# Cross network on one core: VectorE's products spread over the tile, rows and fetches begun earlier, one fp32 chunk where three stood

## The chip, the core and the metric

The kernel runs on one core of a Trainium2 chip. The metric is the device time of one execution in microseconds (us), the median of several runs. Five engines work side by side, each through its own list of instructions in order, and wait for one another on semaphores: TensorE (PE; its weight loads are shown apart as PEld), VectorE (DVE), ScalarE (ACT), GpSimd (POOL) and SyncE (SP), which here only issues DMAs. "SPq" in a row is SP's queue of DMA issues.

## What is computed

512 samples, 39 features each, every feature a row of 16 numbers fetched from its own table. Three layers follow, of 128 maps each, and then a small dense network:

```python
e = stack([tbl_f[ids[:, f]] for f in range(39)])        # (512, 39, 16)
x0 = xk = e
for W in (f0, f1, f2):                                  # (39*39,128), (128*39,128), (128*39,128)
    z = einsum('bfd,bgd->bfgd', x0, xk).reshape(b, f*g, d)
    xk = einsum('bpd,pm->bmd', z, W); outs.append(xk)
h = concatenate([sum(concatenate(outs), -1), dense_ctx], 1)
y = relu(relu(h @ W_top1 + b1) @ W_top2 + b2) @ W_top3  # (512, 1)
```

## The kernel before, in words

**Tiles and slots.** The samples are cut into 16 tiles of 32 samples, which are 512 columns (sample times 16). A tile's second layer is 40 "banks" (`SLOTS`), one for four features of one block of 128 columns; the bank is also the clock of the whole schedule. "Slot s of tile t" (written t:s) is the place of bank 40t+s in each engine's list. What stands at slot s on an engine comes after the engine's work for bank s, in program order; no engine waits for a slot as such, only for its data. `layer2` on TensorE multiplies x1 (split into a high and a low part) with the filter (split as well) in three matmuls, lines 900 to 902, into one of four PSUM buffers (`RING`). Bank n may start when bank n-4 has been read. ScalarE reads banks 0, 3 and 6 of every ten (`scale_bank`, line 594), VectorE the other seven (`add_bank`, line 802: four `scalar_tensor_tensor` per bank, each scaling by a value of x0 and adding to what ScalarE or the bank before left). GpSimd folds a block's sums at slots 8 and 12 of each ten (`fold_two` line 507, `fold_three` lines 514, 516, 520).

**x1 of the next tile** is made beside that. For tile u = t+1 there are seven chunks, each up to three rotations of the 39 feature rows. The path of a chunk: SP loads the turned rows into `z` (line 376); VectorE multiplies them with the plain rows, which ScalarE has copied to PSUM as `three_ps` (`product`, line 749, at slots `CHUNKS_AT`); ScalarE copies the high part (`high_part`, line 553, two slots later); GpSimd subtracts for the low part (`low_part`, line 499, three slots later); TensorE contracts with three matmuls, lines 876, 877 and 882 (eight slots later: slots 8, 12, ..., 32). The last of the three, line 882, is the one that waits for the low part. In tiles 1 to 4 the chunks 1, 3 and 5 are "plain": GpSimd makes the product (line 491, two slots after the chunk's place) and TensorE contracts it as one fp32 matmul (line 873, shown as two records), with no high and low part. Then ScalarE copies x1's high part out of PSUM (slot 34), VectorE subtracts for the low part (`x1_low`, line 755, slot 35) and sums over 16 columns (`sum_x1`, line 783, slot 36; 38 in tile 0). Bank 0 of the next tile waits for both parts of x1. VectorE also transposes x0 for the next tile (`rows`, line 775, slot 30).

**Fetching.** GpSimd gathers the rows of tile u with indirect DMAs (line 481, nine a tile, and line 470 for the five large tables, up to two more a tile), spread evenly over 40 slots that begin 14 slots ahead of tile u-2 (`gathers_at`). So they end near slot 26 of tile u-2. SP stores them to DRAM as they land (lines 390, 397), waits until all are stored, loads them back as x0's rows (`x0_three`, line 428), then issues the turned rows, chunk by chunk, each after the low part of the same chunk of tile u-1, with eight loads for the transposes (line 418) after chunk 2. ScalarE copies `x0_three` to `three_ps` in `three(u)`, at slot 38 of tile u-2 (`THREE_AT`). Within one slot GpSimd's order is: plain product, low part, first fold, second fold, gathers.

From the third group of four tiles on TensorE has extra work: the third layer of the group before (line 918), from slot 19 of tiles 4, 8 and 12 to slot 9 of tiles 7, 11 and 15, then the dense network (lines 929, 960, 967).

Of the kernel before, what the change touches and what calls it, by code (L numbers as in the profile page):

```python
# [26 lines left out]
TILES = GROUPS * TPG  # L27
# [17 lines left out]

TURNED = 20
GATHER_AHEAD = 14

THIRD_TILE_AT = (0, 1, 2, 3, 4, 5, 6, 7, 14, 20)

# [7 lines left out]
C0 = 7  # L58
TURNS = F // 2 + 1


PLAIN = (1, 3, 5)
PLAIN_TILES = range(1, 5)
SEL_REP = 0
SEL_A = FG
# [8 lines left out]
SLOTS = NBLK * BANKS  # L74
# [6 lines left out]

CHUNKS_AT = (0, 4, 8, 12, 16, 20, 24)
FIRST_CHUNKS_AT = (5, 9, 13, 17, 21, 24, 27)
HIGH_LAG = 2
LOW_LAG = 3
PLAIN_LAG = 2
# [3 lines left out]
S_LAG = 25  # L90

LAST_BLOCKS = (TILES * SLOTS - 2 - S_LAG) // BANKS + 1
ROWS_AT = 30
THREE_AT = 38
FIRST_THREE_AT = 4
DIAG_AT = (1, 2, 4, 5, 7, 8, 10, 11)

# [36 lines left out]
def by_act(n):  # L134
    return n % BANKS in BY_ACT
# [23 lines left out]
def chunk_at(u, s, lag):  # L159

    places = FIRST_CHUNKS_AT if u == 1 else CHUNKS_AT
    return places.index(s - lag) if u < TILES and s - lag in places else None


def x1_at(u):
    return FIRST_X1_AT if u == 1 else X1_AT

# [5 lines left out]
def plain(n):  # L173
    return n // C0 in PLAIN_TILES and n % C0 in PLAIN

# [16 lines left out]
def s_block_at(t, s):  # L192

    k = t * SLOTS + s - S_LAG
    return k // BANKS if k >= 0 and k % BANKS == 0 else None
# [15 lines left out]
def gathers_of(u):  # L211

    singles = [(True, g, i) for g, i in singles_of(u)]
    own = [x for x in singles if x[1] == u // TPG]
    return own + [(False, u, i) for i in QUAD_ORDER] + [x for x in singles if x not in own]


def gathers_at(t, s):

    if t == 0 and s in THIRD_TILE_AT:  # L220
        return [x for x, at in zip(gathers_of(2), THIRD_TILE_AT) if at == s]
    found = []
    for u in range(max(3, t + 1), min(t + 4, TILES)):
        first = (u - 2) * SLOTS - GATHER_AHEAD
        x = t * SLOTS + s - first
        if 0 <= x < SLOTS:
            items = gathers_of(u)
            found += items[len(items) * x // SLOTS:len(items) * (x + 1) // SLOTS]
    return found


def cross_network(nc, ids, ids_small, row_numbers, small_tables, tables, w0a, w0b, w1, w1_w, w2, wt1, bt1, wt2, bt2, wt3, dense_t, selectors, identity, mask8, out):
    with ExitStack() as ctx:
# [317 lines left out]
        def _(act):  # L551
# [3 lines left out]
            def spread_rows(t, b):  # L555

                at = slice(32 * (b // 2), 32 * (b // 2) + 32)
                if b == 0:
                    act.wait_ge(rows_in, t + 1)
                    if t >= 2:  # L560
                        act.wait_ge(s_ready, NBLK * (t - 1))
                act.activation(diag[at, t % 2, :, b, :], x0_rows[at, t % 2, :, 0:FS], ACT.Copy,  # L562
                               scale=mask_sb[at, b:b + 1]).then_inc(diag_in, 1)

            def three(u):
                act.wait_ge(three_in[u % 2], 48 * (u // 2 + 1))
                if u > 0:
                    act.wait_ge(prod, split(C0 * u - 1))
                copy(three_ps[0:3 * F, :], x0_three[0:3 * F, u % 2, :]).then_inc(three_up, 1)

            def high_part(u, c):
                n = C0 * u + c
                act.wait_ge(prod, split(n))
                if n >= Z_RING:
                    act.wait_ge(z_done, n - Z_RING + 1)
                k = depth(c)
                copy(z_hi[0:k, n % Z_RING, :], z[0:k, c, :]).then_inc(z_hi_in, 1)

            def x1_high(u):
                act.wait_ge(z_done, C0 * u + C0)  # L580
                if u >= 2:
                    act.wait_ge(y_ready, SLOTS * (u - 1))
                copy(x1_hi[:, u % 2, :], acc0[:, :]).then_inc(x1_hi_in, 1)

            def scale_bank(n):
                k, j = n // BANKS, n % BANKS
                t = k // NBLK
                act.wait_ge(y_ready, n + 1)
                if n % SLOTS == 0:
                    act.wait_ge(rows_in, t + 1)  # L590
                if j == BY_ACT[0] and k >= 2:
                    act.wait_ge(four_in, 2 * (k - 1))
                for i, f in enumerate(fields_of(j)):
                    done = act.activation(scaled[:, k % 2, BY_ACT.index(j), i * M:(i + 1) * M],  # L594
                                          y2[n % RING][:, i * M:(i + 1) * M], ACT.Copy,
                                          scale=x0_rows[:, t % 2, k % NBLK, f:f + 1])
                done.then_inc(y_act, 1)

            def s_out(k):
                act.wait_ge(s_ready, k + 1)  # L600
                g, at = k // (TPG * NBLK), BLK * (k % (TPG * NBLK))
                if at == 0 and g >= 2:
                    act.wait_ge(r3_ready, g - 1)
                if at == 0 and g == 1:
                    act.wait_ge(z_done, C0 * PLAIN_TILES.stop)
                copy(s_sb[:, g % 2, :, at:at + BLK],
                     side[:, 0:BLK * FS].rearrange("p (b f) -> p f b", f=FS)).then_inc(s_in, 1)

            def r2_out(g):
                act.wait_ge(s_in, (g + 1) * TPG * NBLK)  # L610
                if g > 0:
                    act.wait_ge(h1_ready, g)
                copy(r2_sb[:, :], s_sb[:, g % 2, F, :]).then_inc(r2_in, 1)

            def r3_out(g):
                act.wait_ge(r3_ready, g + 1)
                copy(r3_sb[:, :], (y2[0] if g == GROUPS - 1 else late)[:, 0:P]).then_inc(r3_in, 1)

            def h1_out(g):
                act.wait_ge(h1_sum, g + 1)  # L620
                act.activation(h1_sb[:, :, :], h1_sb[:, :, :], ACT.Relu).then_inc(h1_in, 1)
# [56 lines left out]
            for t in range(TILES):  # L678
                g, q = t // TPG, t % TPG
                for s in range(SLOTS):  # L680
                    n = t * SLOTS + s
                    if by_act(n):
                        scale_bank(n)
                    c = chunk_at(t + 1, s, HIGH_LAG)
                    if c is not None and not plain(C0 * (t + 1) + c):
                        high_part(t + 1, c)
                    if t + 1 < TILES and s == x1_at(t + 1):
                        x1_high(t + 1)
                    k = s_block_at(t, s - 1)
                    if k is not None:  # L690
                        s_out(k)
                        if k % (TPG * NBLK) == TPG * NBLK - 1:
                            r2_out(k // (TPG * NBLK))
                    if s in DIAG_AT:
                        spread_rows(t, DIAG_AT.index(s))
                    if t == 0 and s == FIRST_THREE_AT:
                        three(1)
                    if t + 2 < TILES and s == THREE_AT:
                        three(t + 2)
                    if g > 0:  # L700
                        x = q * SLOTS + s
                        if x == L3_AT + L3_SLOTS:
                            r3_out(g - 1)
                        if x == H1_AT + 6:
                            h1_out(g - 1)
                        if x == H2_AT + 2:
                            h2_out(g - 1)
                        if x == Y_AT + 1:
                            y_out_of(g - 1)
# [9 lines left out]
        def _(dve):  # L719
# [24 lines left out]
            def product(u, c):  # L744
                if c == 0:
                    dve.wait_ge(three_up, u + 1)
                dve.wait_ge(a_in[c], rounds(c, u))
                k = depth(c)
                dve.tensor_tensor(z[0:k, c, :], z[0:k, c, :], three_ps[0:k, :], ALU.mult).then_inc(prod, 1)  # L749
# [96 lines left out]
            for t in range(TILES):  # L846
                for s in range(SLOTS):
                    n = t * SLOTS + s
                    if not by_act(n):
                        add_bank(n)  # L850
                    if t >= TPG and t % TPG * SLOTS + s == H1_AT + 4:
                        add_dense(t // TPG - 1)
                    c = chunk_at(t + 1, s, 0)
                    if c is not None and not plain(C0 * (t + 1) + c):
                        product(t + 1, c)
                    if t + 1 < TILES and s == ROWS_AT:
                        rows(t + 1)
                    if t + 1 < TILES and s == x1_at(t + 1) + 1:
                        x1_low(t + 1)
                    if t + 1 < TILES and s == x1_at(t + 1) + 2:  # L860
                        sum_x1(t + 1)
            last_x2(BLOCKS - 1)

# [268 lines left out]
```

## Time and profile before

| | us |
|---|---|
| median of 3 runs (680.06 to 683.67) | 680.94 |
| the profiled execution | 676.92 |
| its span, first to last instruction | 674.9 |
| granted TensorE clock, mean | 0.995 |
| TensorE busy | 636.6 (94%) |
| VectorE busy | 565.5 (84%) |
| GpSimd busy | 533.3 (79%) |
| ScalarE busy | 374.1 (55%) |

The main loop begins at 45.27 us with bank 0 of tile 0. Tile 1 begins at 83.85, tile 2 at 121.14, tile 3 at 158.41, tile 4 at 194.75, tile 8 at 348.30, tile 12 at 501.70 and tile 15 at 614.09; a tile takes 36.3 to 40.7 us. A matmul's record overlaps the next one's, so distances are taken from start to start. Busy shares are means over stages; what a change is worth is read from the starts of single instructions.

### The profile page before, as it was taken

The numbers are of one execution on the slowest core, as the hardware profiler recorded it, in microseconds if no ns is written. First come the engines' busy times: TensorE is split into PE (matmuls) and PEld (weight loads), VectorE is DVE, ScalarE is ACT, GpSimd is POOL, SyncE is SP. The second block draws the span as 40 slices with busy tenths as digits, with TensorE's granted clock in tenths as the row PEclk, the third lists the DMA queues.
The fourth block names the chain that finished last, engine by engine and source line by source line (L and its number), as shares of the span: only waits on it lengthen the run. The fifth ranks groups of instructions, "written<-read, shape, count | busy, mean of one in ns | idle before, by whom it ended". The sixth has DMA issues, their size and how long they took to land.

```text
span 674.9 us, 11454 instructions
## 1 busy us (share of the span) xinstructions
PE 636.6 (94%) x2900; PEld 504.6 (75%) x2900; DVE 565.5 (84%) x1934; ACT 374.1 (55%) x1129; POOL 533.3 (79%) x528
## 2 busy tenths in 40 slices
PE   3388999999999999999999999999999999999998
PEld 1256667777778788888878888888878888887867
DVE  4468888979899898989789898989879898988760
ACT  0445464646556574747467564746557474755431
POOL 6757879999999999998879999897969988574420
PEclk9999999999999999999999999999999999999989
DMA  9535642203241313113230322204031221200000
GB/s 185 112 70 140 211 117 68 62 6 89 40 110 18 98 29 81 44 29 95 43 85 8 84 44 66 60 10 113 10 88 37 63 62 41 81 0 1 2 0 1
DMA packets 79940, 42.25 MB, mean 63 GB/s; under 512 B 56721, under 2 KB 64721, under 8 KB 79746
## 3 DMA queue, kind: packets, MB, share of 16 engines
q1 hardware_dynamic: 67246, 35.85, 20.7%
q10 hardware_dynamic: 7380, 4.38, 3.2%
q0 software_dynamic: 5248, 1.29, 1.9%
q8 instruction: 23, 0.38, 0.2%
q14 instruction: 43, 0.35, 0.2%
HBM read 39.52 MB, written 1.94 MB: 61 GB/s over the span
## 4 chain that ended last, share of the span: by engine, by line
PE 68%; POOL 14%; DVE 5%; issue 5%; SPq 3%; ACT 2%; DMA 2%; POOLq 0%; DVEq 0%
PE y L900 16%; PE y L902 15%; PE y L901 15%; DVE scaled L802 4%; POOL emb_quads L481 4%; PE side L907 4%; PE late L918 4%; PE acc L882 3%; PE acc L877 3%; PE acc L876 3%; POOL sum L514 2%; POOL z_parts L499 2%; POOL sum L507 2%; ACT scaled L594 2%; PE y L918 2%
## 5 line engine op out<-in xcount | busy, mean ns | idle before, releaser
L802 DVE SCALAR_TENSOR_TENSOR scaled<-y,x_rows,scaled 128x128 f32<-128x128 f32 x1728 | 465.4, 341 | 63.4 <-ACT scaled L594 51.7
L594 ACT ACTIVATE scaled<-y,x_rows 128x128 f32<-128x128 f32 x768 | 218.9, 367 | 221.0 <-PE y L902 220.9
L900 PE MATMUL y<-w_hi,x_parts 128*128 128x512 f32 (+1 forms) x640 | 280.5, 438 | 9.5 <-DVE scaled L802 3.4
L902 PE MATMUL y<-w_hi,x_parts 128*128 128x512 f32 (+1 forms) x640 | 248.1, 388 | 0.0
L901 PE MATMUL y<-w_lo,x_parts 128*128 128x512 f32 (+1 forms) x640 | 247.6, 387 | 0.0
L481 POOL DMA_INDIRECT emb_quads<-in_small_tables_dram,quad_rows x144 | 139.2, 967 | 27.4 <-issue 15.6
L900 PEld LDWEIGHTS y<-w_hi,x_parts 128*128 128x128 f32 x640 | 120.6, 188 | 49.6 <-DVE scaled L802 23.0
L499 POOL TENSOR_TENSOR z_parts<-z,z_parts 117x512 fp32r<-117x512 f32 (+1 forms) x95 | 123.3, 1298 | 29.3 <-ACT z_parts L553 28.5
L902 PEld LDWEIGHTS y<-w_hi,x_parts 128*128 128x128 f32 x640 | 120.1, 188 | 24.9
L901 PEld LDWEIGHTS y<-w_lo,x_parts 128*128 128x128 f32 x640 | 121.0, 189 | 20.9 <-issue 2.6
L514 POOL TENSOR_TENSOR sum<-sum,scaled 128x512 f32<-128x512 f32 x63 | 81.7, 1296 | 26.5 <-DVE scaled L802 25.3
L507 POOL TENSOR_TENSOR sum<-scaled 128x512 f32<-128x512 f32 x64 | 83.1, 1298 | 17.9 <-DVE scaled L802 17.4
L553 ACT ACTIVATE z_parts<-z 117x512 fp32r<-117x512 f32 (+1 forms) x100 | 63.7, 638 | 25.2 <-DVE z L749 24.9
L749 DVE TENSOR_TENSOR z<-z,three_ps 117x512 f32<-117x512 f32 (+1 forms) x100 | 67.4, 676 | 6.7 <-DMA z<-x_turned 4.5
L918 PEld LDWEIGHTS late<-s_sb,w_sb 128*128 128x128 f32 x234 | 44.0, 188 | 10.6
L516 POOL TENSOR_TENSOR sum<-sum 128x256 f32<-128x256 f32 x63 | 46.3, 735 | 4.9
L562 ACT ACTIVATE diag<-x_rows,mask_sb 32x160 f32<-32x160 f32 x128 | 49.1, 416 | 1.3
L907 PE MATMUL side<-diag,x_sb 128*128 128x320 f32 x128 | 45.5, 437 | 0.0
L918 PE MATMUL late<-s_sb,w_sb 128*128 128x128 f32 x234 | 44.8, 273 | 0.0
L882 PE MATMUL acc<-z_parts,w_hi 117*128 117x512 f32 (+1 forms) x100 | 40.5, 405 | 0.8 <-POOL z_parts L499 0.5
L876 PE MATMUL acc<-z_parts,w_hi 117*128 117x512 f32 (+1 forms) x100 | 39.8, 398 | 1.2 <-ACT z_parts L553 1.2
L877 PE MATMUL acc<-z_parts,w_lo 117*128 117x512 f32 (+1 forms) x100 | 39.6, 396 | 0.0
(94 smaller groups left out, 376.2 us busy)
## 6 DMA issues: line engine op xcount, KB each, us to landing
z<-x_turned SPq DMA_DIRECT2D x311, 78.0 KB
x_three<-x_turned SPq DMA_DIRECT2D x48, 78.0 KB
x_turned<-emb_quads SPq DMA_DIRECT2D x156, 8.0 KB
w_sb<-in_w_dram SPq DMA_DIRECT2D x1, 2496.0 KB, 9.6
emb_quads<-in_small_tables_dram,quad_rows POOLq DMA_INDIRECT x144, 2.4
s_sb<-in_w_dram ACTq DMA_DIRECT2D x12, 160.0 KB, 5.3
x_turned<-emb_singles SPq DMA_DIRECT2D x89, 2.0 KB
x_turned<-emb_quads SPq DMA_DIRECT2D x64, 2.0 KB
```

Of the source, the lines that this page charges most:

```text
L481: pool.indirect_dma_start(out=emb_quads[0:SPT * n, u % 2, i, :], out_offset=None, in_=packed, in_offset=bass.IndirectOffsetOnAxis(ap=quad_ ...
L499: pool.tensor_tensor(z_lo[0:k, n % Z_RING, :], z[0:k, c, :], z_hi[0:k, n % Z_RING, :].bitcast(F32), ALU.subtract).then_inc(z_lo_in, 1)
L507: pool.tensor_tensor(sum4[:, :], scaled[:, k % 2, 0, :], scaled[:, k % 2, 1, :], ALU.add).then_inc(four_in, 1)
L514: pool.tensor_tensor(sum4[:, :], sum4[:, :], scaled[:, k % 2, 2, :], ALU.add).then_inc(four_in, 1)
L594: done = act.activation(scaled[:, k % 2, BY_ACT.index(j), i * M:(i + 1) * M], y2[n % RING][:, i * M:(i + 1) * M], ACT.Copy, scale=x0_rows[ ...
L749: dve.tensor_tensor(z[0:k, c, :], z[0:k, c, :], three_ps[0:k, :], ALU.mult).then_inc(prod, 1)
L802: dve.scalar_tensor_tensor(part, y2[n % RING][:, i * M:(i + 1) * M], x0_f, part, ALU.mult, ALU.add).then_inc(terms_in, 1)
L900: pe.matmul(dst, x1_hi[:, t % 2, cols], hi, start=True, stop=False)
L901: pe.matmul(dst, x1_hi[:, t % 2, cols], lo, start=False, stop=False)
L902: pe.matmul(dst, x1_lo[:, t % 2, cols], hi, start=False, stop=True).then_inc(y_ready, 1)
L907: pe.matmul(side[:, 0:BLK * FS], x2_sb[:, k % 2, :], diag[:, k // NBLK % 2, k % NBLK, :, :].rearrange("p b f -> p (b f)"), start=True, sto ...
L918: mm = pe.matmul(dst, w2_sb[:, f, :], s_sb[:, g % 2, f, :], start=f == 0, stop=f == F - 1)
```

## The change

VectorE's products for tiles 4 and later no longer stand at slots 0, 4, 8, ..., 24 of tile u-1 but at slots 28 and 32 of tile u-2 and at 1, 6, 10, 15 and 20 of tile u-1. The high and low parts and the contractions keep their slots. The copy to `three_ps` for these tiles moves from slot 38 to 26, their gathers begin 24 instead of 14 slots ahead of tile u-2, the transposes move from slot 30 to 24 for every tile, and `sum_x1` from 36 to 38. In tiles 1 to 4 only chunk 3 stays plain; chunks 1 and 5 are made as elsewhere, at their places in `CHUNKS_AT` for tiles 1 to 3.

```diff
+EARLY_AHEAD = 24
-PLAIN = (1, 3, 5)
+PLAIN = (3,)
+EARLY_FROM = 4
+PRODUCTS_AT = (-12, -8, 1, 6, 10, 15, 20)
+SUM_AT = 38
-ROWS_AT = 30
+ROWS_AT = 24
 THREE_AT = 38
+EARLY_THREE_AT = 26
+def product_at(t, s):
+    for u in (t + 1, t + 2):
+        places = FIRST_CHUNKS_AT if u == 1 else CHUNKS_AT if u < EARLY_FROM else PRODUCTS_AT
+        at = s - SLOTS * (u - 1 - t)
+        if u < TILES and at in places:
+            return u, places.index(at)
+    return None
+def three_at(u):
+    return EARLY_THREE_AT if u >= EARLY_FROM else THREE_AT
@@ gathers_at
-        first = (u - 2) * SLOTS - GATHER_AHEAD
+        first = (u - 2) * SLOTS - (EARLY_AHEAD if u >= EARLY_FROM else GATHER_AHEAD)
@@ scalar
-                    if t + 2 < TILES and s == THREE_AT:
+                    if t + 2 < TILES and s == three_at(t + 2):
                         three(t + 2)
@@ vector
-                    c = chunk_at(t + 1, s, 0)
-                    if c is not None and not plain(C0 * (t + 1) + c):
-                        product(t + 1, c)
+                    due = product_at(t, s)
+                    if due is not None and not plain(C0 * due[0] + due[1]):
+                        product(*due)
-                    if t + 1 < TILES and s == x1_at(t + 1) + 2:
+                    if t + 1 < TILES and s == SUM_AT:
                         sum_x1(t + 1)
```

## Rows read from the trace of the kernel before

**Rows 1.** The page's first part: busy us, share of the span, instructions.
```profile
PE 636.6 (94%) x2900; PEld 504.6 (75%) x2900; DVE 565.5 (84%) x1934; ACT 374.1 (55%) x1129; POOL 533.3 (79%) x528
```
**Rows 2.** Who waited for whom: us in total, times, longest us.
```profile
PEld y L900 <- DVE scaled L802: 23.0, 59, 1.0
...
PEld acc L882 <- POOL z_parts L499: 4.8, 11, 1.0
```
**Rows 3.** Timeline of PE, tile 3: start us, us, engine, line, names [idle before].
```profile
169.50 0.39 PE L901 MATMUL y<-w_lo,x_parts 128*128 128x512 f32 x1
...
171.04 0.40 PE L901 MATMUL y<-w_lo,x_parts 128*128 128x512 f32 x1
...
187.70 0.39 PE L901 MATMUL y<-w_lo,x_parts 128*128 128x512 f32 x1
...
188.40 0.40 PE L901 MATMUL y<-w_lo,x_parts 128*128 128x512 f32 x1
...
189.79 0.39 PE L901 MATMUL y<-w_lo,x_parts 128*128 128x512 f32 x1
```
**Rows 4.** Timeline of PE where tile 8 begins: banks 8:0, 8:1, 8:5, 8:6.
```profile
348.30 0.40 PE L900 MATMUL y<-w_hi,x_parts 128*128 128x512 f32 x1
...
349.69 0.50 PE L900 MATMUL y<-w_hi,x_parts 128*128 128x512 f32 x1 [0.52 <-DVE scaled L802]
...
353.12 0.50 PE L900 MATMUL y<-w_hi,x_parts 128*128 128x512 f32 x1
...
354.22 0.64 PE L900 MATMUL y<-w_hi,x_parts 128*128 128x512 f32 x1
```
**Rows 5.** Timeline of DVE at the same place.
```profile
347.32 0.68 DVE L755 TENSOR_TENSOR x_parts<-acc,x_parts 128x512 fp32r<-128x512 f32 x1
347.92 0.68 DVE L783 TENSOR_REDUCE r_sb<-acc 128x32 f32<-128x512 f32 x1
348.51 2.93 DVE L802 SCALAR_TENSOR_TENSOR scaled<-y,x_rows,scaled 128x128 f32<-128x128 f32 x11
351.36 0.67 DVE L749 TENSOR_TENSOR z<-z,three_ps 117x512 f32<-117x512 f32 x1
```
**Rows 6.** Timeline of DVE, slots 28 to 34 of tile 2.
```profile
151.91 0.49 DVE L775 STREAM_TRANSPOSE x_rows<-x_quarters 128x128 f32<-128x128 f32 x2
...
155.34 0.35 DVE L802 SCALAR_TENSOR_TENSOR scaled<-y,x_rows,scaled 128x128 f32<-128x128 f32 x1 [0.65 <-ACT scaled L594]
```
**Rows 7.** Timeline of POOL, slots 24 to 32 of tile 1.
```profile
106.71 1.31 POOL L499 TENSOR_TENSOR z_parts<-z,z_parts 117x512 fp32r<-117x512 f32 x1
107.95 1.30 POOL L491 TENSOR_TENSOR z<-z,x_three 117x512 f32<-117x512 f32 x1
109.20 1.28 POOL L514 TENSOR_TENSOR sum<-sum,scaled 128x512 f32<-128x512 f32 x1
...
111.98 0.98 POOL L470 DMA_INDIRECT emb_singles<-in_tbl_dram,ids_sb  x1
...
114.22 1.32 POOL L499 TENSOR_TENSOR z_parts<-z,z_parts 78x512 fp32r<-78x512 f32 x1
```
**Rows 8.** Timeline of PE, tile 1: the contractions of chunks 5 and 6.
```profile
111.74 1.02 PE L873 MATMUL acc<-z,s_sb 117*128 117x512 f32 x2
...
115.67 0.42 PE L882 MATMUL acc<-z_parts,w_hi 78*128 78x512 f32 x1
```
**Rows 9.** Timelines of PE and POOL: waits for a part, tiles 2 and 8.
```profile
145.33 0.50 PE L882 MATMUL acc<-z_parts,w_hi 117*128 117x512 f32 x1 [0.55 <-POOL z_parts L499]
...
357.11 1.30 POOL L499 TENSOR_TENSOR z_parts<-z,z_parts 117x512 fp32r<-117x512 f32 x1 [0.59 <-ACT z_parts L553]
```
**Rows 10.** Timelines of ACT, POOL, SP: from a last gather to x0's rows.
```profile
86.33 0.60 ACT L553 ACTIVATE three_ps<-x_three 117x512 f32<-117x512 f32 x1 [3.63 <-DMA x_three<-x_turned]
...
529.35 0.95 POOL L481 DMA_INDIRECT emb_quads<-in_small_tables_dram,quad_rows  x1 [0.15 <-issue]
...
533.02 1.15 SPq L428 DMA_DIRECT2D x_three<-x_turned  x3
```

## The prediction

> **What bounds the kernel now.** I read the busy shares first. TensorE is busy 636.6 of 674.9 us, VectorE and GpSimd stand at 84% and 79% [rows 1], so TensorE's stream sets the length, but two others are close enough to hold it up in places. The list of waits says by whom: TensorE's queue waits 23.0 us in 59 short waits for VectorE to free a bank, and 4.8 us in 11 waits for a low part from GpSimd [rows 2]. The timelines then say where. An undisturbed bank takes 0.70 us from one L901 to the next [rows 3]. Where tile 8 begins, bank 8:1 starts 1.39 us after 8:0, and from 8:0 to 8:6 it is 5.92 us [rows 4]; five banks of 0.70 and one of 1.10 (353.12 to 354.22, with the side matmuls behind it) would be 4.60. So about 1.3 us are lost there to VectorE. The same pattern, 1.3 to 1.5 us, stands where tiles 2, 3, 4 and 12 begin; where TensorE has other work in the slots, tiles 5 to 7, 9 to 11 and 13 to 15, I count 0.3 to 0.6. All from tile 3 on is some 9 us, 1.4% of the run, and that is the most that respacing VectorE's work could win. GpSimd's stalls are the second item: 0.8 us at 2:24 (start of L882 at 145.33 after a wait of 0.55 [rows 9]), 0.4 at each of 1:24, 2:20, 3:20 and 4:28, and 0.2 to 0.3 at slot 28 of tiles 5, 8, 9 and 12.
>
> **Part 1: fp32 chunks into split ones.** With a plain chunk between them, two L901 stand 171.04 - 169.50 = 1.54 us apart, with a split chunk 189.79 - 188.40 = 1.39, without either 188.40 - 187.70 = 0.70 [rows 3]. A plain chunk so costs TensorE 0.84, a split one 0.69; each exchange saves 0.15. Eight are exchanged, two in each of tiles 0 to 3: 1.2 us. The two in tile 0 win nothing, since in tile 1 everything waits for x0's rows at 86.33 [rows 10], a transfer that SP issues at its own pace. That leaves 0.9. VectorE gets eight products at 0.6 each (347.92 to 348.51 is the step of an operation of that size [rows 5]), 4.8 us; ScalarE eight high parts. On GpSimd a subtraction takes the place of each product, 1.30 against 1.31 [rows 7], at nothing. VectorE's products fall at slots 9 and 24 of tile 0 and 4 and 20 of tiles 1 and 2, where it waits for ScalarE's bank, as it does for 0.65 us at 155.34 [rows 6]; I take nothing, with 0 to 1.5 us as bounds (nothing hidden at two of the eight). For tile 4 they fall in the new places.
>
> **A place that matters more:** a plain product stands before the second fold in slot 22, the low part of chunk 5 behind it in slot 23. The fold and its two halves take 111.98 - 109.20 = 2.8 us [rows 7]. So chunk 5 of tiles 2, 3 and 4 is ready 2.8 us later than now.
>
> **Part 2: products and sum respaced.** Two products go into slots 28 and 32. In tile 2 VectorE is done with the transposes at 152.36 or so and then waits, 0.65 us alone before 155.34 [rows 6]; the transposes (0.45 us) leave this stretch as well. Each product, 0.6, fits a hole, so x1's low part isn't late. At the tile's beginning I follow VectorE's queue. Now it is: x1's low part 347.32, sum 347.92, banks 7:37, 7:38, 7:39 from 348.51, product 351.36, then 8:1 and 8:2 [rows 5], without a gap. Afterwards it is: low part, 7:37, 7:38, sum, 7:39, 8:1, product, 8:2. The same nine items end at the same time. A bank takes VectorE 1.03 us. So 8:1 may start at 349.1 instead of 349.69, 8:2 at 350.1, but 8:3 waits for 7:39, done as before near 351.5, and 8:6 waits for 8:2, done at 354.1 as before. TensorE reaches 8:6 at 354.16 instead of 354.22 [rows 4]. I take 0.05 us for each of 12 beginnings, 0.6 us in all. The stall moves from the first bank to the third and isn't shorter, because the work of VectorE in front of bank 8:2 is the same.
>
> **Part 3: gathers ten slots earlier.** From tile to tile their density is the same, so in the steady state they cost nothing. But tile 3 keeps its old place (slots 26 of tile 0 to 26 of tile 1) and tile 4 begins at slot 16 of tile 1. In slots 16 to 25 of tile 1 both are gathered, and three of tile 4's (slots 19, 23 and 26) come in front of the low part of chunk 6. GpSimd has no gap there: low part 106.71, plain 107.95, fold 109.20, and so on to the low part at 114.22 [rows 7], whose end near 115.47 TensorE needs at 115.67 [rows 8]. There is 0.2 us to spare. An inserted gather costs 1.2 us (a low part followed by a gather steps 1.43, a gather 0.97, less the 1.25 saved). The ledger: chunk 1 of tile 2, now split, waits for ScalarE's high part, +0.5 for all that follows; low part of chunk 4 at 107.2; gather 108.65; fold 109.6; gather 112.4; low part of chunk 5 at 113.4, ready at 114.7. TensorE would want it at 112.7 (it contracts chunk 5 at 111.74 now [rows 8], the third matmul 0.46 later, +0.5): it waits 2.0 us. Then gathers at 114.85, 116.1, 117.35, low part of chunk 6 at 118.3, ready at 119.6, wanted at 118.1: 1.5 us. With the delay at chunk 4 and the saving of the exchange, tile 1 is 3.9 us longer. Bounds: 2 us if VectorE's and GpSimd's present slack takes half, 5.5 if the quad gathers step by 1.3 and tile 2 starts as late again.
>
> The Trainium skill says of GpSimd, in "Perfetto Trace Analysis", section "GPSIMD Engine Instruction", that the recorded spans don't add up and that start-to-start distances are to be used. The rows show what that changes: by recorded lengths three gathers would be 3 x 0.96 = 2.9 us, by steps they are 3.5; the tile would come out 0.6 us shorter by lengths.
>
> **What the shift gives back.** In tiles 2, 5 and 9 one gather fewer stands in front of the low part of chunk 5, and in tile 3 and 4 the gather in slot 1 no longer delays the fold. And with products made early, ScalarE's high part of chunk 1 is in time: GpSimd now waits 0.59 us for it at 357.11 [rows 9] and then works without a gap to slot 28. So the waits at 4:28 (0.4), 5:28 and 9:28 (0.3 each), 8:28 and 12:28 (0.2 each) go: 1.4 us. Tile 2: the wait at 2:24 (0.8) goes, that at 2:20 grows by 0.3, one of 0.4 comes at 2:28, exchange 0.3: 0.4 gained. Tile 3: 0.4 at 3:20 and the exchange, 0.7 gained.
>
> **Is the data there?** ScalarE's copy at slot 26 now stands in front of its banks. Today tile 14's last gather begins at 529.35 and the load of x0's rows is issued at 533.02 [rows 10], 3.7 us later; three issues and the landing take some 2.8. That is 6.5 us from the last gather's start. Its new place is slot 15; GpSimd runs 3 to 4 slots late, and ScalarE comes to slot 26 about 2 us after TensorE: 7 slots of 0.93 and 2 are 8.5 us. It holds, with 2 us in tile 12 and under 1 in tile 2. No price.
>
> **The sum**, against the profiled 676.92 us: +3.9 (tile 1), -0.4 (tile 2), -0.7 (tile 3), -1.4 (waits for low parts), -0.6 (beginnings) = +0.8, so 677.7, or +0.12%. On the median of 680.94, 0.6% above the profiled run, that is 681.7 us. A measurement of this kernel can hardly tell 0.5% (3.4 us) from no change. The likeliest case's own range is 679 to 684.
>
> **Rivals.**
> - *The beginnings of the tiles get free.* If VectorE's products at slots 0 and 4 are what fills the ring, then with them gone the 9 us from tile 3 on go too: 681.7 - 9 = 673, half of it 677. For it speaks that these waits are by far the most [rows 2]. Against it: a product remains in slot 1, in front of bank 8:2. 0.16.
> - *The overlap of gathers costs little*, because TensorE's waits let GpSimd catch up and the order of chunks 5 and 6 hides it: 3.9 us fall to about 1, 678.8. The slack of 0.2 us [rows 8] speaks against it. Still within 0.5%. 0.16.
> - *Slower: the early copy waits for its rows.* If the last gather begins later than slot 20, its 6.5 us reach past ScalarE's slot 26, ScalarE stands with all its banks behind it, and TensorE with the ring after four more. It decides at 2 us more lateness of GpSimd than now. At 0.5 us for each of 12 tiles it is 6 us, 687.7. GpSimd's lateness of 3 slots in tile 12 speaks for it, as does the tight place in tile 2. With it goes a dearer tile 1, 5.5 us. 0.18.
> - *The forecast*: 0.50.
>
> Range 676 to 686.5: it takes in half of the first rival and the nearer part of the slower one. Faster by over 0.5% (under 677.5) 0.18, within 0.5% 0.63, slower (over 684.3) 0.19.
>
> **What would show it.** In the trace after: L882 of chunks 5 and 6 in tile 1 after waits of 1.5 to 2 us for L499, tile 2 beginning near 125 instead of 121.14; where tile 8 begins, 8:1 on time, 8:3 late, and 8:0 to 8:6 still 5.8 to 5.9 us; no wait at slot 28 in tiles 5, 8, 9; no ScalarE wait for x0's rows after tile 1; two L901 around chunk 1 of tile 2 1.39 us apart. I am wrong if 8:0 to 8:6 comes under 5.2, or if tile 1 keeps its 37.3 us.

## The result: 0.8% slower, inside the range, but almost seven times the forecast's loss

The changed kernel takes 686.1 us (median of 18 runs, 682.8 to 690.6) against 680.7 us (median of 18 runs of the kernel before, 678.2 to 684.3). The ratio is 1.0078, 95% interval 1.0057 to 1.0099: 5.4 us slower. The forecast was 681.7, 0.12% slower than before, in a range of 676 to 686.5. The range holds by 0.4 us; the likeliest case's own range, 679 to 684, missed it. With the interval wholly above 1.005, the outcome is "slower", which had a chance of 0.19, and not "within 0.5%", which had 0.63.

The page after, first part and TensorE's clock in 40 slices:

```profile
PE 635.8 (93%) x2908; PEld 506.7 (74%) x2908; DVE 570.3 (84%) x1942; ACT 376.9 (55%) x1137; POOL 533.9 (78%) x528
...
PEclk9969999899999999999999999999999999999999
```

The shares are those of before [rows 1] to within a point. VectorE has 4.8 us more (eight products at 0.6) and GpSimd 0.6. TensorE is busy 0.8 us less in a span that is 7.4 us longer, so it idles more. The span must be cut before it is read. Bank 0 of tile 0 starts at 50.34 instead of 45.27 us, in code that the change doesn't touch: TensorE ran at half clock from 35.2 to 45.5 us. In the eleven profiles of variants with the same code there, that start lies between 44.9 and 51.5 us. From tile 15's first bank to the end it is 58.1 instead of 60.8 us, since the profile of before has a half-clock stretch of 6.8 us there. Neither belongs to the change. What is left is tiles 0 to 14: 573.9 us instead of 568.8, 5.1 us more, which fits the 5.4 us between the medians. Their lengths, from the start of one tile's bank 0 to the next one's, with the experiments' in the same columns:

```
tile    before  after plain_only gathers_only sum_36 three_27 from_eight sum_next sum_slot_2 free_front
 0       38.58  38.24   39.68      38.37      39.12   38.40    38.08     38.68     39.48      39.62
 1       37.29  41.46   38.40      46.45      40.73   44.22    41.52     38.84     37.47      44.41
 2       37.26  36.84   37.57      35.29      36.82   36.82    37.59     37.29     37.33      36.85
 3       36.35  36.16   36.41      35.99      36.15   36.17    36.45     36.41     36.41      35.93
 5       37.79  37.68   37.79      37.52      37.50   37.67    39.29     37.53     37.53      37.22
 6       37.53  37.92   37.51      37.54      37.52   37.91    37.94     37.49     37.40      37.30
 7       40.70  41.37   40.71      40.66      41.18   40.81    41.37     40.47     40.39      40.75
 8       37.36  37.31   37.35      37.45      37.24   37.27    37.27     37.10     37.01      36.75
 4-14   419.3  421.2   419.2      418.7      419.0   420.0    422.9     417.5     416.8      415.7
```

From tile 2 on the figures repeat to a few hundredths between profiles where nothing is changed. In tiles 0 and 1 they don't, because TensorE's clock falls to half there in 12 of the 13 profiles, at varying places.

**Tile 1.** Timeline of TensorE after the change, at slots 28 to 31 of tile 1 (L897, L898 and L903 are the contraction, 876, 877 and 882 before; L921 is 900):

```profile
117.32 0.40 PE L898 MATMUL acc<-z_parts,w_lo 117*128 117x512 f32 x1
119.61 0.50 PE L903 MATMUL acc<-z_parts,w_hi 117*128 117x512 f32 x1 [1.90 <-POOL z_parts L520]
119.95 0.34 PE L921 MATMUL y<-w_hi,x_parts 128*128 128x384 f32 x1
...
120.47 0.56 PE L921 MATMUL y<-w_hi,x_parts 128*128 128x512 f32 x1
120.83 0.63 PE L922 MATMUL y<-w_lo,x_parts 128*128 128x512 f32 x1
121.25 0.63 PE L923 MATMUL y<-w_hi,x_parts 128*128 128x512 f32 x1
121.68 0.63 PE L921 MATMUL y<-w_hi,x_parts 128*128 128x512 f32 x1
```

The third matmul of chunk 5 starts 2.29 us after the second instead of 0.23: 2.06 us of waiting for GpSimd. Right after it the matmuls stand 0.42 us apart instead of 0.23. GpSimd at that place, which [rows 7] answer to:

```profile
112.08 1.29 POOL L520 TENSOR_TENSOR z_parts<-z,z_parts 117x512 fp32r<-117x512 f32 x1
113.52 0.96 POOL L491 DMA_INDIRECT emb_singles<-in_tbl_dram,ids_sb  x1 [0.16 <-issue]
114.50 1.30 POOL L535 TENSOR_TENSOR sum<-sum,scaled 128x512 f32<-128x512 f32 x1
...
117.31 0.96 POOL L491 DMA_INDIRECT emb_singles<-in_tbl_dram,ids_sb  x1
118.28 1.28 POOL L520 TENSOR_TENSOR z_parts<-z,z_parts 117x512 fp32r<-117x512 f32 x1
```

Low part of chunk 4, tile 4's gather, the fold with its halves, tile 3's gather, and only then the low part of chunk 5, 6.20 us after that of chunk 4: in the order of the ledger, which had 6.2. From its bank 6 to its end tile 1 takes 34.46 us instead of 30.51, 3.95 us more. The clock of two stretches around it (the window; its us; busy by engine; PEclk; DMA share; GB/s):

```profile
112.00:118.00 6.00, 5.18 (x21) 3.50 (x19) 4.55 (x18) 2.89 (x10) 5.51 (x7) 1.00 0.25 41
120.50:123.90 3.40, 3.40 (x10) 2.65 (x9) 1.56 (x6) 1.14 (x4) 2.78 (x4) 0.51 0.41 101
```

**The beginnings of tiles.** VectorE and ScalarE before the change, where tile 6 begins (ScalarE's row is bank 36):

```profile
268.42 0.68 DVE L755 TENSOR_TENSOR x_parts<-acc,x_parts 128x512 fp32r<-128x512 f32 x1
269.01 0.68 DVE L783 TENSOR_REDUCE r_sb<-acc 128x32 f32<-128x512 f32 x1
269.61 2.92 DVE L802 SCALAR_TENSOR_TENSOR scaled<-y,x_rows,scaled 128x128 f32<-128x128 f32 x11
```

```profile
268.15 1.15 ACT L594 ACTIVATE scaled<-y,x_rows 128x128 f32<-128x128 f32 x4 [1.43 <-PE y L902]
```

VectorE, ScalarE and TensorE there after it, the pattern that now stands in tiles 6, 10 and 14:

```profile
276.33 0.68 DVE L776 TENSOR_TENSOR x_parts<-acc,x_parts 128x512 fp32r<-128x512 f32 x1
277.32 2.16 DVE L823 SCALAR_TENSOR_TENSOR scaled<-y,x_rows,scaled 128x128 f32<-128x128 f32 x8 [0.30 <-issue]
279.39 0.68 DVE L804 TENSOR_REDUCE r_sb<-acc 128x32 f32<-128x512 f32 x1
```

```profile
276.07 1.14 ACT L615 ACTIVATE scaled<-y,x_rows 128x128 f32<-128x128 f32 x4 [1.43 <-PE y L923]
```

```profile
278.00 0.40 PE L921 MATMUL y<-w_hi,x_parts 128*128 128x512 f32 x1
...
280.90 0.51 PE L921 MATMUL y<-w_hi,x_parts 128*128 128x512 f32 x1 [0.41 <-DVE scaled L823]
```

x1's low part steps 0.60 us (347.32 to 347.92 in [rows 5]), so VectorE was free at 276.93, and went on at 277.32. ScalarE's record of bank 36 ends at 277.21, and bank 37 adds to it. The row names no releaser (`issue`), but such a hole stands in front of nine tiles, and in all nine VectorE goes on 0.10 us after the end of ScalarE's record. Before the change the sum stood in the hole. The sum, L804, now stands two banks later, and bank 39 ends 0.4 us later against the start of the tile than before. Bank 6:3 waits for that.

Where tile 8 begins there is no hole. TensorE's banks 8:0 to 8:3 after the change:

```profile
357.28 0.40 PE L921 MATMUL y<-w_hi,x_parts 128*128 128x512 f32 x1
...
358.06 0.50 PE L921 MATMUL y<-w_hi,x_parts 128*128 128x512 f32 x1
...
359.10 0.50 PE L921 MATMUL y<-w_hi,x_parts 128*128 128x512 f32 x1
...
360.47 0.50 PE L921 MATMUL y<-w_hi,x_parts 128*128 128x512 f32 x1 [0.42 <-DVE scaled L823]
```

### The profile page after: what moved, and what is told of

The parts are those of the page before. It is cut to its first block, busy times and chain, and to the rows that moved or that the text cites. A ratio compares the mean times of both kernels' runs of the same rounds, so it can differ in the third digit from the quotient of the medians.

```text
span 682.3 us, 11494 instructions
## 1 busy us (share of the span) xinstructions
PE 635.8 (93%) x2908; PEld 506.7 (74%) x2908; DVE 570.3 (84%) x1942; ACT 376.9 (55%) x1137; POOL 533.9 (78%) x528
## 4 chain that ended last, share of the span: by engine, by line
PE 58%; DVE 12%; POOL 11%; issue 10%; SPq 4%; ACT 3%; DMA 1%; POOLq 0%; DVEq 0%; ACTq 0%
PE y L921 14%; PE y L923 13%; PE y L922 13%; DVE scaled L823 10%; PE side L928 3%; PE late L939 3%; POOL emb_quads L502 3%; PE acc L903 3%; ACT scaled L615 3%; PE acc L898 3%; PE acc L897 3%; POOL sum L528 2%; SPq L418 2%; POOL sum L535 2%; POOL z_parts L520 1%
## 5 line engine op out<-in xcount | busy, mean ns | idle before, releaser
L823 DVE SCALAR_TENSOR_TENSOR scaled<-y,x_rows,scaled 128x128 f32<-128x128 f32 x1728 | 466.8, 344 | 64.1 <-ACT scaled L615 40.3
L921 PE MATMUL y<-w_hi,x_parts 128*128 128x512 f32 (+1 forms) x640 | 276.4, 432 | 11.7 <-DVE scaled L823 5.7
L520 POOL TENSOR_TENSOR z_parts<-z,z_parts 117x512 fp32r<-117x512 f32 (+1 forms) x103 | 133.6, 1297 | 37.0 <-ACT z_parts L574 36.3
L921 PEld LDWEIGHTS y<-w_hi,x_parts 128*128 128x128 f32 x640 | 120.9, 189 | 50.1 <-DVE scaled L823 21.7
L923 PEld LDWEIGHTS y<-w_hi,x_parts 128*128 128x128 f32 x640 | 120.5, 188 | 25.0
L770 DVE TENSOR_TENSOR z<-z,three_ps 117x512 f32<-117x512 f32 (+1 forms) x108 | 73.1, 678 | 8.1 <-DMA z<-x_turned 6.3
L574 ACT ACTIVATE z_parts<-z 117x512 fp32r<-117x512 f32 (+1 forms) x108 | 69.0, 639 | 11.0 <-DVE z L770 9.0
L903 PE MATMUL acc<-z_parts,w_hi 117*128 117x512 f32 (+1 forms) x108 | 44.6, 413 | 4.9 <-POOL z_parts L520 3.1
L897 PE MATMUL acc<-z_parts,w_hi 117*128 117x512 f32 (+1 forms) x108 | 43.5, 403 | 1.9 <-ACT z_parts L574 1.9
L928 PE MATMUL side<-diag,x_sb 128*128 128x320 f32 x128 | 44.9, 432 | 0.0
L898 PE MATMUL acc<-z_parts,w_lo 117*128 117x512 f32 (+1 forms) x108 | 43.7, 404 | 0.0
```

What stands on the lines that cost most here:

```text
L520: pool.tensor_tensor(z_lo[0:k, n % Z_RING, :], z[0:k, c, :], z_hi[0:k, n % Z_RING, :].bitcast(F32), ALU.subtract).then_inc(z_lo_in, 1)
L574: return act.activation(dst, src, ACT.Copy)
L823: dve.scalar_tensor_tensor(part, y2[n % RING][:, i * M:(i + 1) * M], x0_f, part, ALU.mult, ALU.add).then_inc(terms_in, 1)
L921: pe.matmul(dst, x1_hi[:, t % 2, cols], hi, start=True, stop=False)
L923: pe.matmul(dst, x1_lo[:, t % 2, cols], hi, start=False, stop=True).then_inc(y_ready, 1)
```

## The experiments

Each was timed against the kernel before in the same set of runs; the ratio comes with its 95% interval. "Slots 28 to 34" is the distance from bank 28's start to bank 34's.

### Each part alone

**plain_only**, the kernel before with one edit:

```diff
-PLAIN = (1, 3, 5)
+PLAIN = (3,)
```

> The kernel before with only chunk 3 left plain in tiles 1 to 4. Theory (the place in GpSimd's queue decides): the low part of chunk 5 now stands behind the second fold of slot 22, so TensorE waits for it once in each of tiles 1, 2 and 3, by 0.8, 0.85 and 0.5 us, and for chunk 4 of tile 1 by 0.5 more; the exchanges give back 0.15 us each, 0.9 in tiles 1 to 3. Tile 1 becomes about 1.0 us longer, the whole run 1 to 1.8 us, ratio 1.0015 to 1.0026. Rival (TensorE's own work decides, an fp32 chunk being dearer than a split one): the eight exchanges shorten the run by 0.9 to 1.2 us, ratio 0.998, and tile 1 is no longer than 37.3 us.

Measured: ratio 1.0036, 1.0016 to 1.0057. Slots 28 to 34 of tiles 1, 2 and 3 take 6.35, 6.32 and 6.02 us instead of 5.59, 5.59 and 5.54: 0.76, 0.73 and 0.48 more, where 0.8, 0.85 and 0.5 less 0.15 of the exchange were expected. The waits of TensorE in the timeline, chunks 4 and 5 of tile 1, then of tile 2, then chunk 5 of tile 3:

```profile
109.18 0.50 PE L882 MATMUL acc<-z_parts,w_hi 117*128 117x512 f32 x1 [0.55 <-POOL z_parts L499]
...
114.17 0.51 PE L882 MATMUL acc<-z_parts,w_hi 117*128 117x512 f32 x1 [0.70 <-POOL z_parts L499]
...
146.78 0.50 PE L882 MATMUL acc<-z_parts,w_hi 117*128 117x512 f32 x1 [0.56 <-POOL z_parts L499]
...
151.77 0.50 PE L882 MATMUL acc<-z_parts,w_hi 117*128 117x512 f32 x1 [0.70 <-POOL z_parts L499]
...
188.16 0.50 PE L882 MATMUL acc<-z_parts,w_hi 117*128 117x512 f32 x1 [0.37 <-POOL z_parts L499]
```

The theory holds, the rival falls: less work on TensorE, and the run isn't shorter. Tiles 1 to 3 are 1.5 us longer. Of the rest of the ratio, tile 0's 1.1 us came with a half-clock stretch at 55.9 us in this profile, and isn't shown to be the change's.

**gathers_only**, the kernel before with

```diff
-        first = (u - 2) * SLOTS - GATHER_AHEAD
+        first = (u - 2) * SLOTS - (24 if u >= 4 else GATHER_AHEAD)
```

> The kernel before with only the gathers of tile 4 and later begun 24 instead of 14 slots ahead. Theory (two tiles' gathers overlap in tile 1 and three of them come in front of the low part of chunk 6): TensorE waits 3 to 3.5 us for that part, tile 1 is 40.3 to 40.8 us long instead of 37.3; later some 1.5 to 2 us come back at slots 24 and 28 of tiles 2, 3, 5 and 9; the run is 1.3 to 2 us longer, ratio 1.002 to 1.003. Rival (GpSimd's slack takes the overlap): tile 1 grows by under 1 us and the run is 1 us shorter, ratio 0.998.

Measured: ratio 1.0037, 1.0005 to 1.0068. In tile 1 TensorE waits for the low part of chunk 6:

```profile
124.55 0.55 PE L882 MATMUL acc<-z_parts,w_hi 78*128 78x512 f32 x1 [3.40 <-POOL z_parts L499]
```

That bank is 3.7 us longer than before the change, a little over the 3 to 3.5 expected. Slots 28 to 34 of tiles 5 and 9 fall from 6.13 to 5.84 us, as expected, and tile 2 from 37.26 to 35.29. The rival, under 1 us in tile 1 and a shorter run, falls. Tile 1's length missed: 46.45 us instead of 40.3 to 40.8; this profile has half-clock stretches at 90.7 (6.8 us) and at 124.9 (3.4 us), the second right behind the wait.

**respace_only**, the changed kernel with `PLAIN = (1, 3, 5)`.

> The changed kernel with chunks 1, 3 and 5 plain as before: respacing and earlier fetches alone. Theory: all but the low part of chunk 5 stays as in the changed kernel; tile 1 about 40.5 us (gathers), beginnings of tiles 6, 10 and 14 0.4 us longer than before, the run 4 us longer than before, ratio 1.005 to 1.007. Rival (the exchange of the fp32 chunks made the loss): ratio 1.000 to 1.002.

Measured: ratio 1.0102, 1.0067 to 1.0136. Respacing and fetching alone lose what the whole change loses, 573.9 us in tiles 0 to 14 in both profiles, so the rival, that the exchange made the loss, falls. That the ratio should be above the whole change's isn't clear of the intervals. Beside the rest the exchange isn't free everywhere: with it tiles 2 and 3 take 36.84 and 36.16 us, without it 35.89 and 35.80, and tile 1 gives that back. Tile 1 took 42.9 us here, expected 40.5: its one long wait stands in slot 32, with the half clock at 120.6 behind it, and banks 33 to 35 take 3.95 us instead of 2.36. Tiles 6, 10 and 14 take 5.63 us from bank 0 to bank 6, 0.39 more than before.

### The sum's place

**sum_36**, the changed kernel with the sum back behind x1's low part:

```diff
-                    if t + 1 < TILES and s == SUM_AT:
+                    if t + 1 < TILES and s == x1_at(t + 1) + 2:
                         sum_x1(t + 1)
```

> The changed kernel with the sum of x1 back in slot 36. Theory (bank 37 has to wait for ScalarE's bank 36, the sum used to fill that hole and now stands where there is none): from bank 0 to bank 6 tile 6 takes 5.25 us again instead of 5.62, tiles 10 and 14 the same, tiles 5, 9 and 13 lose 0.18 less each; 2 us in all against the changed kernel, ratio to the kernel before 1.004 to 1.006. Rival (the early products in slots 28 and 32 make VectorE late): tile 6 still takes 5.6 us from bank 0 to bank 6, ratio as for the changed kernel, 1.0078.

Measured: ratio 1.0051, 1.0027 to 1.0075. Bank 0 to bank 6 takes 5.23 us in tile 6 (273.62 to 278.85), in tiles 10 and 14 too, and tiles 4 to 14 are 2.2 us shorter than in the changed kernel. Two products at slots 28 and 32 are there as before, so they cost nothing; the sum's move did. This run told something else as well. No half-clock stretch fell in its tile 1, and TensorE waits for both chunks there:

```profile
115.46 0.50 PE L903 MATMUL acc<-z_parts,w_hi 117*128 117x512 f32 x1 [1.89 <-POOL z_parts L520]
...
120.33 0.50 PE L903 MATMUL acc<-z_parts,w_hi 78*128 78x512 f32 x1 [1.30 <-POOL z_parts L520]
```

From bank to bank these are 2.17 and 1.59 us lost, where the prediction had 2.0 and 1.5. Slots 28 to 34 take 9.12 us, in the changed kernel with its half-clock stretch 9.14. The low part of chunk 6 sets that end, and slower matmuls in front of it only fill the time in which TensorE would have waited. In respace_only no wait followed, and the half clock cost its 1.6 us.

**sum_next** and **sum_slot_2**: the kernel before, and only the sum moved, to slot 4 or 2 of the next tile.

```diff
-                    if t + 1 < TILES and s == x1_at(t + 1) + 2:
-                        sum_x1(t + 1)
+                    if t > 0 and s == 4:
+                        sum_x1(t)
```

> The kernel before with one edit: the sum of x1 in slot 4 of the next tile instead of slot 36 of its own, so behind VectorE's first banks there. Theory (at a tile's beginning the work of VectorE in front of bank 2 is what TensorE waits for): bank 0 to bank 6 takes 5.35 us in tiles 2, 3, 4, 8 and 12 instead of 5.91, and 4.95 to 5.0 in tiles 5, 6, 9, 10, 13 and 14 instead of 5.2; up to 0.35 us of it comes back in slots 6 to 9 where the sum now stands; in all 3 to 6 us faster, ratio 0.991 to 0.996. Rival (TensorE there waits for ScalarE's banks and VectorE's share doesn't matter): 5.9 us stay, ratio 1.000.

Measured: ratio 0.9966, 0.9937 to 0.9995. TensorE where tile 8 begins, banks 8:0, 8:1, 8:2 and 8:6, for [rows 4]:

```profile
355.72 0.40 PE L900 MATMUL y<-w_hi,x_parts 128*128 128x512 f32 x1
...
356.50 0.50 PE L900 MATMUL y<-w_hi,x_parts 128*128 128x512 f32 x1
...
357.53 0.50 PE L900 MATMUL y<-w_hi,x_parts 128*128 128x512 f32 x1
...
361.05 0.64 PE L900 MATMUL y<-w_hi,x_parts 128*128 128x512 f32 x1
```

5.33 us instead of 5.92; 4.91 to 5.04 in tiles 5, 6, 9, 10, 13 and 14. So it is VectorE's work in front of bank 2 that counts: one operation of 0.6 us less, 0.6 us less. In slots 8 and 9, where the contraction waits for the sum, 0.2 to 0.4 us come back, under 0.1 in tiles 5, 9 and 13. Tiles 4 to 14 are 1.8 us shorter, so the 3 to 6 us expected in all were too much, and the ratio isn't in the 0.991 to 0.996 named.

> The kernel before with the sum of x1 in slot 2 of the next tile, behind bank 2, where VectorE waits for ScalarE's bank 3, and two slots sooner than in the run with slot 4, where the contraction in slot 8 had to wait for it. Theory: bank 0 to bank 6 takes 5.3 us in tiles 2, 3, 4, 8 and 12 and 4.9 to 5.05 in tiles 5 to 7, 9 to 11, 13 to 15, and nothing comes back at slot 8; tiles 1 to 14 are 5 to 6 us shorter than before, ratio 0.991 to 0.993. Rival (the wait for the sum just moves to another bank): tiles 1 to 14 no shorter than with slot 4, ratio 0.9966.

Measured: ratio 0.995, 0.9925 to 0.9976, the lowest here, though its interval overlaps that of slot 4. The beginnings are as with slot 4. In slots 8 and 9 the loss is 0.07 us in tiles 6, 7, 10 and 11 instead of 0.17, but 0.28 in tiles 8 and 12, so "nothing comes back" was too much. Tiles 4 to 14 are 2.5 us shorter than before. Tiles 2 and 3 gain nothing in length: with TensorE earlier at the front, the wait for GpSimd's plain product at slot 20 grows from 0.4 to some 0.85 us. The 5 to 6 us expected left that out.

**free_front**, the changed kernel with the sum in slot 4 of the next tile and

```diff
-PRODUCTS_AT = (-12, -8, 1, 6, 10, 15, 20)
+PRODUCTS_AT = (-12, -8, 6, 9, 12, 16, 20)
```

> The changed kernel with the sum in slot 4 of the next tile and the later products at slots 6, 9, 12, 16 and 20 instead of 1, 6, 10, 15 and 20, so that only x1's low part is left in VectorE's queue between bank 35 of a tile and bank 2 of the next. Theory: from tile 3 on bank 0 to bank 6 takes 4.6 us in tiles 3, 4, 8 and 12 and 4.9 in the others, 8 to 10 us less in all than in the changed kernel, in spite of the long tile 1; ratio to the kernel before 0.992 to 0.997. Rival (the wait only moves on, to the contraction in slot 8 that needs the sum, or to the banks behind the products): the sum of tiles 4 to 14 stays within 2 us of the changed kernel's 424.2 us.

Measured: ratio 0.9993, 0.9971 to 1.0015. Tiles 4 to 14 take 415.7 us instead of 421.2 (the text above names 424.2, a wrong addition), so the rival falls; but 5.5 us were gained and not 8 to 10, and the ratio isn't in the 0.992 to 0.997 expected. Bank 0 to bank 6 takes 4.91 to 5.02 us in the tiles with extra work on TensorE, as expected, and 5.05 to 5.09 in tiles 3, 4, 8 and 12, not 4.6. There banks 8:1 and 8:2 are still 0.2 and 0.35 us late: the low part alone, with banks 37 to 39 behind it, keeps VectorE late.

### The copy in front of the dense layer

Not foreseen: slots 28 to 34 of tiles 7 and 11 went from 6.13 to 6.65 us. ScalarE and TensorE at 7:29 in the changed kernel:

```profile
347.48 0.61 ACT L574 ACTIVATE three_ps<-x_three 117x512 f32<-117x512 f32 x1
348.00 0.62 ACT L657 ACTIVATE h_sb<-late,bt_sb 128x128 f32<-128x128 f32 x2
```

```profile
348.68 0.60 PE L988 MATMUL late<-h_sb,wt_sb 128*1 128x128 f32 x4 [0.50 <-ACT h_sb L657]
```

The copy to `three_ps`, now in slot 26, runs just before the output of the second dense layer of the same slot, and TensorE needs that in slot 29. **three_27** is the changed kernel with `EARLY_THREE_AT = 27`.

> The changed kernel with ScalarE's copy to three_ps in slot 27 instead of 26, so behind the copy of the second dense layer in slot 26 of tiles 7 and 11. Theory (the copy stands in front of h2_out and TensorE waits for that in slot 29): slots 28 to 34 of tiles 7 and 11 take 6.13 us as before the change instead of 6.65, all other tiles as in the changed kernel; 1.0 us less than the changed kernel. Rival (the early product in slot 28 makes the waits there): 6.6 us stay.

Measured: 6.11 us in both tiles, all other tiles from 2 on as in the changed kernel; tiles 4 to 14 1.2 us shorter. Ratio 1.0062, 1.0032 to 1.0093, whose interval overlaps that of the changed kernel; that 1.0 us is won is read from the tiles.

### The overlap in another place, and in steps

**from_eight** is the changed kernel with `EARLY_FROM = 8`.

> The changed kernel with the early places for tiles 8 and later instead of 4 and later; the gathers of two tiles now overlap in slots 16 to 25 of tile 5, where TensorE has the third layer's matmuls between the banks. Theory (the overlap has one price, set by how much GpSimd has to spare at that place): tile 1 falls to 38.4 us, tile 5 grows by about 2.2 us to 40.0 (1.4 us for chunk 5, 1.0 for chunk 6, less the 0.3 there now), and no half-clock stretch of TensorE follows in tile 5 if its waits stay near 1 us each; the run stays some 5 us over the kernel before, ratio 1.006 to 1.009. Rival (tile 1 is long because of what follows from the start of the run, not because of the overlap): tile 1 stays above 40 us and tile 5 at 37.7.

Measured: ratio 1.0067, 1.0041 to 1.0094. Slots 28 to 34 fall to 6.34 us in tile 1 and rise to 7.44 in tile 5:

```profile
271.18 0.50 PE L903 MATMUL acc<-z_parts,w_hi 117*128 117x512 f32 x1 [1.20 <-POOL z_parts L520]
...
274.84 0.50 PE L903 MATMUL acc<-z_parts,w_hi 78*128 78x512 f32 x1
```

The overlap follows the edit. It costs 1.5 us at chunk 5 (1.4 expected), and only 0.1 at chunk 6 (1.0 expected): tile 5 is 39.29 us, not 40.0. No half clock follows. Tile 1 is long all the same, 41.5 us, as the rival had: half-clock stretches fell at 51.8 and 96.1 us, the second behind the wait for x0's rows at its beginning. Behind that, from bank 8 of tile 1 to its end, it takes 30.0 us, as in plain_only, where the changed kernel takes 32.8. So the overlap's 2.8 us have left tile 1, and the rival's reason falls.

**gathers_in_steps**, the kernel before with

```diff
-        first = (u - 2) * SLOTS - GATHER_AHEAD
+        first = (u - 2) * SLOTS - (GATHER_AHEAD + 2 * min(max(u - 4, 0), 5))
```

> The kernel before with the gathers begun 16, 18, 20, 22 and 24 slots ahead for tiles 5, 6, 7, 8 and 9 and later, so that the ten slots are won over five tiles instead of one. Theory (an inserted gather costs only where GpSimd's part is already awaited; GpSimd idles elsewhere in each tile): no wait at slot 28 or 32 over 0.6 us, tiles 3 to 7 within 0.4 us of before, ratio 0.998 to 1.001. Rival (each of the three gathers brought forward has its price of 1.2 us wherever it stands): 3.5 us more, ratio 1.005.

Measured: ratio 0.999, 0.9959 to 1.0022. Tiles 2 to 14 are 1.5 us longer in all, not 3.5; the edit doesn't reach tile 1. Single places missed: tile 3 is 0.9 us longer (a wait at slot 32), tile 5 0.6, where at most 0.4 was expected. Spread out, most of the price goes, but not all of it.

**in_steps_and_sum** puts together gathers in steps, early products from tile 9 on (slots 28, 32, 4, 8, 12, 16, 20), the copy in slot 27, three plain chunks and the sum in slot 2.

> Chunks 1, 3 and 5 plain as before, gathers brought forward in steps over tiles 5 to 9, from tile 9 on products at slots 28 and 32 and at 4, 8, 12, 16 and 20, the copy to three_ps in slot 27, the sum in slot 2 of the next tile. Theory: as the run with the sum in slot 2 up to tile 7; from tile 8 on VectorE has no product in front of bank 2 either, and bank 0 to bank 6 takes 4.6 to 5.0 us everywhere; 6 to 7 us less than the kernel before, ratio 0.989 to 0.992. Rival (the early places cost more than they give, beside the sum): ratio at or above that of the sum in slot 2 alone.

Measured: ratio 0.9959, 0.9925 to 0.9992, no better than the sum in slot 2 alone; that much of the rival stands. From bank 0 to bank 6 tile 8 takes 5.13 us and the later ones 4.91 to 5.06, a little over the 4.6 to 5.0 expected. From tile 8 to 14 it takes 262.5 us against 263.9 with the sum alone, and in tiles 3 to 5 it loses 2.1 us to the gathers brought forward. What the early products give, the road to them takes.

## Why the prediction was right and where not, step by step

| step | forecast, us | measured, us |
|---|---|---|
| tiles 0 and 1 | +3.9 | +3.8 |
| tile 2 | -0.4 | -0.4 |
| tile 3 | -0.7 | -0.2 |
| beginnings of tiles 4 to 15 | -0.6 | +1.9 |
| waits for low parts, slots 28 to 34, tiles 4 to 14 | -1.4 | -0.7 |
| dense layer, tiles 7 and 11 | none | +1.0 |
| sum | +0.8 | +5.4; tiles 0 to 14 show +5.1 |

The sign came from tile 1, as forecast. The size was missed by 4.6 us: outside tile 1 the forecast had 3.1 us of gains, and 1.6 us of losses came. That the time is still in the range is luck: the range was drawn for other rivals, and none of them happened.

**Tile 1 was right for its reasons.** The ledger's two waits, 2.0 and 1.5 us, are 2.17 and 1.59 in the run without a half-clock stretch. That an inserted gather costs 1.2 us and not its recorded 0.96 stands in the rows: the steps are 1.44 and 0.98 (112.08, 113.52, 114.50), less the 1.24 of a low part by itself (106.71 to 107.95 in [rows 7]). The Trainium skill's advice to take start-to-start distances on GpSimd ("Perfetto Trace Analysis", section "GPSIMD Engine Instruction") agrees with this trace. What the sum left out is that TensorE falls to half clock for 3.4 us behind such a wait in five of six profiles with the overlap in tile 1. In the changed kernel that cost nothing of its own, since a wait would have followed.

**The part that said "the stall moves and isn't shorter" was right for tile 8 and wrong for most.** From 8:0 to 8:6 it is 5.85 us instead of 5.91 to 5.92, forecast 0.05 less, and 8:3 is the late one, as written. The step that failed is the one that carried this to 12 tiles: "the same nine items end at the same time", "without a gap". In tiles 4, 8 and 12 ScalarE's bank 36 ends before VectorE needs it. In the nine others it doesn't, and the sum used to fill that hole; moved, it left the hole empty and stood in front of bank 39 at its full price. The holes behind x1's low part are 0.17 us in tiles 5, 9 and 13, 0.38 in 6, 10 and 14 and 0.15 in 7, 11 and 15. The beginnings of these tiles are longer by 0.17, 0.38 and 0.16; tiles 4, 8 and 12 gain 0.06. The rows of tile 6 were in the trace and weren't followed. Putting the sum back (sum_36) returned 2.2 us.

**The wait of 0.59 us for a high part [rows 9] was put down to the product alone.** With the product long done, GpSimd still waits 0.35 us there after the change, for ScalarE's own queue. The waits at slots 28 and 32 of tiles 4, 8 and 12 stayed, 0.15 to 0.35 us a tile, where the forecast let them go. That ScalarE's queue alone keeps them isn't shown: sum_next has the wait for the high part in tile 8 too, 0.61 us, and none at 8:28. There GpSimd's fold for bank 39 starts 2.61 us after the tile and not 3.22, as it does before and after the change. At 5:28 and 9:28 the waits went as forecast, in gathers_only as well, so by the earlier gathers. In tile 3 a wait left slot 20 and one of 0.6 us came at slot 28: GpSimd's chain was as long as before, its low part stood behind the fold.

**One queue wasn't asked.** The prediction weighed the copy at slot 26 by whether its data was there, and not by what stands behind it on ScalarE in that slot. That is 1.0 us, shown by three_27.

**Part 1** was right in its parts: the exchange saves 0.15 us a chunk (banks 12 and 13 of tile 2 take 2.10 us instead of 2.24), and the chunk's place behind the fold costs 0.5 to 0.8 in tiles 1 to 3. For the first two tiles of the run, the forecast that a saving there is swallowed can't be told apart from clock stretches.

**The rivals.** "The beginnings get free" didn't happen: the product moved from slot 0 to 1 is still in front of bank 2. sum_next and free_front show that its mechanism is real: take work out of that stretch and TensorE is sooner. "The overlap costs little" fell. The slower rival, the copy waiting for its rows, didn't happen: after tile 1 ScalarE never waits for x0's rows.

## What to carry to other kernels

Respacing an engine's work pays only if the work leaves the stretch in front of the item that the next engine waits for; inside it, every order has the same sum, except that an operation may stand in a hole, which costs nothing until it is moved out. A pattern read in one tile must be read in each kind of tile before it is multiplied by their number. And of an operation that moves, ask what stands behind it in every queue, also where its data is early.

## What the runs showed of the hardware

TensorE's granted clock fell to half (0.50 to 0.51 in a window, matmuls of 512 columns 0.42 us apart instead of 0.23) for 3.4 or 6.8 us at a time, once for 10.2, the end of the run aside. In the changed kernel it came at 120.5 us, right behind a wait of 2.1 us; in the 6 us from 112 to 118 TensorE was busy 5.18. With the overlap in tile 1 such a stretch followed the wait in five profiles and didn't in a sixth, sum_36, with the same wait of 2.2 us. Behind a wait of 1.5 us in tile 5 none came. What decides it in a single execution is open; nothing here was made to test it. Its share in the spread between executions (682.8 to 690.6 us at mean clocks of 0.983 to 0.995) is seen, but not separated.
